# Reordering the second half of a dense feed-forward and the entry to the next attention layer, on all engines of a two-layer transformer kernel

## The reference

```
x = x + ffn(attention(x, ...))                    # layer 1
x = x + experts(attention(x, ...))                # layer 2

def attention(x, ...):                            # 16 heads of 64, one key and value for all heads
    xn = ln(x); q = xn @ Wq; k, v = split(xn @ Wkv)   # a null key and value are put in front
    sim = q @ k + bias, masked causally and by key
    return layernorm(softmax(sim) @ v @ Wout)

def ffn(x, ln1_g, ln1_b, w1, b1, ln2_g, ln2_b, w2, b2):
    h = layer_norm(x, ln1_g, ln1_b)
    h = h @ ternary_quant(w1).T + b1              # 128 -> 512
    h = gelu(h)
    h = layer_norm(h, ln2_g, ln2_b)               # over the 512
    return h @ ternary_quant(w2).T + b2           # 512 -> 128
```

## Time and profile before

| | before |
|---|---|
| time, median of 3 runs | 584.27 us (584.1 to 586.46) |
| span of the profiled execution, which is the time that its rows add up to | 586.0 us |
| mean granted TensorE clock | 0.934 |
| PE busy | 483.6 us (83%) |
| DVE busy | 426.4 us (73%) |
| ACT busy | 377.5 us (64%) |
| POOL busy | 312.0 us (53%) |

### The profile page before, as it was taken

The page is one execution under the profiler, slowest core; times in us unless marked ns, Lnnn a source line. Parts: engine busy times, 40 slices in busy tenths (PEclk is TensorE's granted clock), DMA queues, the critical chain, the costliest instruction groups (busy, mean ns, idle before and its releaser), DMA issues.

```text
span 586.0 us, 13781 instructions
## 1 busy us (share of the span) xinstructions
PE 483.6 (83%) x3220; PEld 390.9 (67%) x3220; DVE 426.4 (73%) x2148; ACT 377.5 (64%) x1475; POOL 312.0 (53%) x368
## 2 busy tenths in 40 slices
PE   3768999999999888987899999989987229999930
PEld 1456777777777676666788887867865217878730
DVE  4899999999999786577778888899887604343413
ACT  1568889888888866655888898868774004354410
POOL 4577666675657725567333453534675522555560
PEclk9689999999999989999899999999998659999975
DMA  5361016621100000000022120000111121323117
GB/s 170 93 180 22 20 26 137 141 78 45 41 4 6 8 3 2 0 1 7 6 65 58 44 77 5 8 7 15 37 38 31 40 68 36 84 53 83 36 38 215
DMA packets 54696, 29.73 MB, mean 51 GB/s; under 512 B 19884, under 2 KB 51572, under 8 KB 54644
## 3 DMA queue, kind: packets, MB, share of 16 engines
q1 hardware_dynamic: 48900, 22.09, 15.1%
q0 software_dynamic: 2560, 4.90, 2.6%
q10 hardware_dynamic: 3184, 2.16, 1.2%
HBM read 16.13 MB, written 10.90 MB: 46 GB/s over the span
## 4 chain that ended last, share of the span: by engine, by line
PE 59%; DVE 12%; issue 11%; POOL 6%; ACT 4%; DMA 4%; SPq 1%; another core or an unknown queue 1%; DVEq 0%; ACTq 0%; POOLq 0%
PE psS L863 10%; PE psA L918 7%; PE psS L1162 5%; PE psQ L834 4%; PE psT L881 4%; PE psO L899 4%; PE psQ L818 4%; PE psQ L1152 3%; PE psO L889 2%; DVE sc L1557 2%; PE psO L890 2%; DMA slot_rows<-Y,dest_u 1%; ACT qT L1248 1%; PE psO L1152 1%; PE psA L1152 1%
## 5 line engine op out<-in xcount | busy, mean ns | idle before, releaser
L1265 ACT ACTIVATE sc<-sc,negmax 128x97 f32<-128x97 f32 (+3 forms) x512 | 179.0, 354 | 23.7 <-DVE negmax L1557 22.1
L634 POOL TENSOR_TENSOR wide_buf<-bias,mask 128x132 f32<-128x132 f32 (+3 forms) x128 | 109.2, 877 | 9.2 <-DMA bias<-rel_scratch 3.9
L1557 DVE CUSTOM_DVE_ANT_0 sc<-psS,wide_buf 128x97 f32<-128x97 f32 (+3 forms) x512 | 93.6, 237 | 25.6 <-PE psS L863 18.4
L863 PE MATMUL psS<-kk,qT 128*128 128x194 f32 (+3 forms) x512 | 102.7, 322 | 11.6 <-DVE negmax L1557 11.6
L863 PEld LDWEIGHTS psS<-kk,qT 128*128 128x128 f32 x512 | 80.0, 195 | 33.0 <-issue 30.0
L1265 ACT ACTIVATION_READ_ACCUMULATOR sc<-sc,negmax 128x1 f32 x512 | 97.3, 190 | 0.0
L581 POOL TENSOR_TENSOR qrn<-qssc,half 128x9 f32<-128x9 f32 (+1 forms) x32 | 55.9, 1748 | 57.8 <-DVE qssc L1543 57.7
L1570 DVE TENSOR_TENSOR pn<-sc,rsum 128x128 f32<-128x128 f32 (+3 forms) x128 | 72.4, 566 | 6.8 <-DVE rsum L1566 0.2
L918 PE MATMUL psA<-Wo,OT 128*128 128x128 f32 (+1 forms) x512 | 65.7, 283 | 0.8 <-DVE OT L1582 0.8
L918 PEld LDWEIGHTS psA<-Wo,OT 128*128 128x128 f32 x512 | 62.7, 196 | 2.0 <-DVE OT L1582 1.8
L1582 DVE TENSOR_SCALAR OT<-psO,cols 128x512 f32<-128x512 f32 x64 | 47.6, 743 | 3.3 <-PE psO L899 1.8
(11 more groups left out here) (298 smaller groups left out, 1014.9 us busy)
## 6 DMA issues: line engine op xcount, KB each, us to landing
slot_rows<-empty SPq DMA_DIRECT2D x2, 1390.0 KB, 10.0
xb<-slot_rows SPq DMA_DIRECT2D x16, 139.0 KB
vp_u<-vp SPq DMA_DIRECT2D x128, 8.0 KB, 1.7
choice_rows<-zero_row SPq DMA_DIRECT2D x8, 256.0 KB, 3.2
wide_buf<-choice_rows SPq DMA_DIRECT2D x8, 256.0 KB, 5.0
vp_u<-vp SPq DMA_DIRECT2D x64, 16.0 KB, 1.8
eW<-in_L_ffn_W SPq DMA_DIRECT2D x4, 256.0 KB, 3.1
gT<-in_L_ffn_W SPq DMA_DIRECT2D x4, 256.0 KB, 3.0
```

The source lines that it names most:

```text
L634: pool.tensor_tensor(unit_masked(i, u).rearrange("p h e k -> p (h e) k"), unit_bias(layer, u).rearrange("p h e k -> p (h e) k"), mask[laye ...
L863: m = pe.matmul(score_bank(u, h), qT[i][:, h, u].rearrange("p m q -> p (m q)"), kk[i][:, :, 0:w], start=True, stop=True)
L1265: m = act.activation(v, v, ACT.Exp, bias=negmax[:, u, g:g + 1], scale=-1.0, accum_out=psum_row[:, u, g:g + 1])
L1557: dve.tensor_tensor_reduce(sc[u][:, h, e, :], score_bank(u, h)[:, e * WIDTH[u]:(e + 1) * WIDTH[u]], unit_masked(i, u)[:, h, e, :], -1.0, - ...
```

## The change

The same instructions are issued, on other tiles of PSUM in four cases, and in another order on four engines; SP's program is as before. By engine:
- PE: f_up(0, 1) to f_up(0, 3) and f_turn(1) are spread between the last projection of layer 1 and the two preparations. Of the last quad, two f_downs stay ahead of layer 2, f_down(14) goes behind b0's scores of u1 and f_down(15) behind those of u2; project_in for b1 follows it, turn_input for b2 comes behind u3. The last quad's tiles go to halves of psO and of one bank of psT, since psS then holds scores. A wait for all 16 reads stands ahead of b1's scores; the wait for 14 ahead of layer 2 is gone.
- ACT: f_in of the next quad one step earlier; in b0 the keys and queries of b1 behind u2's exponentials.
- DVE: dense_stats(3) ahead of the copies of the gate; f_norm_in(3) ahead of f_update(0); f_read(3) in two halves in b0's u2 and u3; f_update(3) and f_input_stats(3) in b1.
- POOL: the addition of c to X in four pieces spread through the program; the mask additions for b0 and f_input_rstd(0) ahead of quad 2's sums; the later f_input_rstds and f_scale(3) later.

```
 # PE
+            f_up(0, 1)
             project(0, NB - 1, 1, False)
...
+            f_up(0, 2)
+            pe.wait_ge(s["out_ready"], 2 * NB)
+            down_sums()
+            f_up(0, 3)
+            f_turn(1)
+            gate_fold()
...
             turn_input(1, 1, 1)
-            for t in range(NB - 4, NB):
-                f_down(t)
-            project_in(1, 1)
-            pe.wait_ge(s["f_o_read"], NB - 2)
+            f_down(NB - 4)
+            f_down(NB - 3)
 # PE, f_bank and f_down
+            if t >= NB - 4:
+                c = (t % 2) * (P + 2)
+                return (psO[:, c:c + P + 2], psT[:, 1, c:c + P + 2])[(t % 4) // 2]
...
-                held(pe, s["f_o_read"], t - 3)
+                held(pe, s["f_o_read"], t - 3 if t < NB - 4 else NB - 5 + (t % 4) // 2)
 # PE, batches of layer 2
+                    if no(b, 1):
+                        pe.wait_ge(s["f_o_read"], NB)
                     for u in range(UNITS):
                         scores(1, b, u, i)
+                        if first and u in (1, 2):
+                            f_down(NB - 3 + u)
+                        if first and u == 2:
+                            project_in(1, 1)
+                        if first and u == 3:
+                            turn_input(1, 2, 0)
 # ACT
+                    if j == FB - 1 and g < QUADS - 1:
+                        f_in(g + 1)
                     f_square(g, j)
-                if g < QUADS - 1:
-                    f_in(g + 1)
 # DVE
+            f_norm_in(2)
+            f_read(0)
+            f_norm_in(3)
+            f_update(0)
+            f_input_stats(0)
...
+                        if first and u == 2:
+                            values_in(1, 1, 1)
+                            f_read(QUADS - 1, 0, 2)
+                        if first and u == 3:
+                            f_read(QUADS - 1, 2, 4)
+                        if u == 1 and no(b, 1):
                             f_update(QUADS - 1)
-                        if first and u == 2:
+                        if u == 2 and no(b, 1):
                             f_input_stats(QUADS - 1)
 # POOL
+            f_pair_sum(0, 0)
+            f_shift(0)
+            f_pair_sum(0, 1)
+            f_square_sum(0)
             dense_rstd(QUADS - 1)
...
+            f_shift(1)
+            f_squares(1)
+            f_scale(0)
             pool.wait_ge(s["masks_ready"], 2)
             for u in range(UNITS):
                 mask_bias(1, 0, u, 0)
+            f_input_rstd(0)
+            f_squares(2)
+            f_shift(2)
+            f_scale(1)
+            f_squares(3)
+            f_scale(2)
             values_set(1, 0, 0)
...
+            f_shift(3)
+            f_input_rstd(1)
+            f_input_rstd(2)
```

More of the change, by code:

```diff
@@ L728, in f_input_rstd @@
                 rsqrt(rstd[:, 4 * g:4 * g + 4], ve[:, 4 * g:4 * g + 4], 4, s["x_rstd"])
+            f_pair_sum(0, 0)
+            f_shift(0)
+            f_pair_sum(0, 1)
+            f_square_sum(0)
             dense_rstd(QUADS - 1)
-            for g in range(QUADS):
-                f_squares(g)
-                if g:
-                    f_scale(g - 1)
-                if g and g < QUADS - 1:
-                    f_input_rstd(g - 1)
+            f_shift(1)
+            f_squares(1)
+            f_scale(0)
             pool.wait_ge(s["masks_ready"], 2)
@@ L1019, in batch @@
                             values(B - 1, 1 - i)
-                        if u == 2 and not last and not no(b, NB - 2):
+                        if u == 2 and not first and not last and not no(b, NB - 2):
                             turn_input(1, b + 2, i)
@@ L1101, in _ @@
             f_up(0, 0)
+            f_up(0, 1)
             project(0, NB - 1, 1, False)
-            for g in range(QUADS):
-                for j in range(FB):
-                    if g or j:
-                        f_up(g, j)
-                    if g == 0 and j == 0:
-                        pe.wait_ge(s["out_ready"], 2 * NB)
-                        down_sums()
-                    if g == 0 and j == 1:
-                        gate_fold()
+            f_up(0, 2)
[4 more added lines that the diff above has]
+            gate_fold()
+            for g in range(1, QUADS):
+                for j in range(FB):
+                    f_up(g, j)
                     if g == 1 and j == 1:
@@ L1116, in _ @@
                         f_turn(g + 1)
-                    if g and j:
+                    if j:
                         f_down(4 * (g - 1) + j - 1)
-                if g:
-                    f_down(4 * g - 1)
+                f_down(4 * g - 1)
             pe.wait_ge(s["y_done"], NB)
@@ L1329, in batch @@
                     for u in range(UNITS):
-                        if u == 0 and not last:
+                        if u == 0 and not first and not last:
                             keys_T(1, b + 1, 1 - i)
@@ L1336, in batch @@
                         weights(n + u, u)
-                        if u == 1 and not last:
+                        if u == 2 and first:
+                            keys_T(1, 1, 1)
+                        if u == (2 if first else 1) and not last:
                             queries(1, b + 1, 1 - i)
@@ L1949, in f_input_stats @@
                 dve.tensor_scalar(ve[:, quad], mv[:, quad, 1], LN_EPS, None, ALU.add).then_inc(s["x_var"], 1)
-            for g in range(QUADS - 1):
-                if g + 2 < QUADS:
-                    f_norm_in(g + 2)
-                if g == QUADS - 2:
-                    null_keys(cols[:, C_NK:C_NK + 1])
-                    dve.wait_ge(s["x_rstd"], 1)
-                    input_norm(1, 0, 0)
-                    input_norm(1, 1, 1)
-                f_read(g)
-                if g == QUADS - 2:
-                    values_in(1, 0, 0)
-                f_update(g)
-                f_input_stats(g)
-            f_read(QUADS - 1)
-            dve.wait_ge(s["x_rstd"], QUADS - 2)
+            f_norm_in(2)
[3 more added lines that the diff above has]
+            f_input_stats(0)
+            f_read(1)
+            f_update(1)
+            f_input_stats(1)
+            null_keys(cols[:, C_NK:C_NK + 1])
+            dve.wait_ge(s["x_rstd"], 1)
+            input_norm(1, 0, 0)
+            input_norm(1, 1, 1)
+            f_read(2)
+            values_in(1, 0, 0)
+            f_update(2)
+            f_input_stats(2)
             attention_second()
```

40 lines of the change are left out of this document (23 added, 17 removed).

## The result

| | before | after |
|---|---|---|
| median (lowest to highest) | 584.28 us (582.37 to 588.21), 20 runs | 580.07 us (578.42 to 586.48), 20 runs |
| ratio to before, 95% interval | | 0.994 (0.9921 to 0.9958) |
| span of the profiled execution, granted clock | 586.0 us, 0.934 | 578.3 us, 0.943 |

The change is 4.2 us faster by the medians, 3.5 by the ratio (2.5 to 4.6 by its interval); forecast were 3.2, and 581.0 us.

What follows compares the result with a forecast made beforehand. The prediction took PE's standing still or running slowly, in the feed-forward and b0, to be what counts. Its terms, 0 + 4.2 + 1.0 − 2.0, gave 3.2 us gained, 581.0 us on the median, range 578.0 to 584.8.

Steps and rivals of the forecast that it cites:

- Term 1: Feed-forward up to turn_input(1,0,0): 0; PE's closed holes are given back by POOL; bounds 3.1 gained to 0.4 lost.
- Term 2: From turn_input to b0's first scores: 4.2 us gained, as two f_downs and project_in(1) leave this stretch.
- Term 3: Batch b0: 1.0 us gained, moved work filling PE's idle time and the clock staying up; bounds 1.9 gained, 0.6 lost.
- Term 4: b1 and b2: 2.0 us lost, from f_update(3) and f_input_stats(3) on DVE in b1; bounds 0 to 2.9, or 4.3.
- Rival (c): Layer 2's entry: clock falls behind new PE holes of 1.7 and 2.4; 583.3, or 588.2 if through b0; chance 0.13.
- (a): Feed-forward and b1: update and masks overlap better, b1 absorbs half; gain 4.5 to 7 us, about 578.5; chance 0.22.

Runs made afterwards that it cites:

- e1: Changed kernel with only the new entry; the feed-forward on PE, ACT, DVE and POOL back in the old order; 584.13 us, 0.9996 of before.
- e7: Changed kernel plus matrix products nobody reads in PE's two waits, ahead of f_down(8)'s second product and b0's turn_input; 580.56 us, 0.9931 of before.
- e10: Kernel before plus 14 matrix products nobody reads in b0's PE wait of 3.99 us; 586.06 us, 1.0039 of before.
- e3: Changed kernel with b0's four mask additions on POOL behind quad 2's sums, f_input_rstd(0), f_scale(1) and a piece of X+c; 583.11 us, 0.9978 of before.
- e8: Changed kernel with f_update(3) moved on DVE from b1's to b2's u1 and f_input_stats(3) to b3's u1; 581.03 us, 0.9956 of before.
- e4: Changed kernel with f_down(12) ahead of b1's turn_input on PE and b0's queries ahead of b1's xnT on ACT; 580.92 us, 0.9933 of before.
- e5: e3 with null_keys and both input_norms ahead of f_update(1) on DVE, and values_in(b0) ahead of f_read(2); 579.34 us, 0.9916 of before.
- e6: e5 with f_input_stats(2) moved behind b0's second bias step and f_input_rstd(2) on POOL behind b1's values; 578.09 us, 0.9909 of before.
- e12: e6 with f_update(3) in b2, f_input_stats(3) in b3, and f_scale(3) on POOL behind b2's masks; 577.48 us, 0.9882 of before.

## Why the prediction was right, point by point

By the trace the mechanism stood in its main lines, and the sum of 3.2 met 3.7 by the trace and 4.2 by the medians. That it came so near is partly luck: terms 2, 3 and 4 were off by 0.8, 0.95 and 0.5, and the first offset half of the other two. And e1's median, with the same entry and no gain, leaves open why the medians show the whole. Term by term:

- Term 1, 0 forecast, 0.16 lost. Its steps are in the trace one by one: quad 3 begun 4.66 earlier (4.3 forecast), f_update(0) 3.02 under the masks (3.08), a wait of 1.87 for POOL's sum (1.7), turn_input at 39.69 after f_up(0,0) against 39.53. One step fell elsewhere: the 1.2 for quad 3's pair sums was not on f_update(1), which ran alone, but on the two xn (2.60 for 0.60), and the second hole was 0.88 and not 2.4, because the clock had fallen in the first. The page "SBUF — State Buffer" of the Trainium skill, section "Who interferes with whom", whose rule weighed for this end, was borne out: the four updates and the four masks took 3.02 and 3.09 side by side, as if in turns.
- Term 2, 4.2 forecast, 3.4 gained. The work that left was right; the 0.3 for PE reaching ACT's copies too soon was too small, the row shows 0.89, and its cause was not PE coming early but DVE's copy of the values coming late, behind the slow xn. e1 and e7, without that wait, have 5.42 and 5.53, just the 5.4 of the sum.
- Term 3, 1.0 forecast, 1.95 gained. The left-over waits were 0.31 and 0.24, not 0.8, and the clock stayed up, as assumed. e10 measures the clock's part by itself: 1.6. Against e10's b0 of 10.91 the 4.54 us of PE's work that moved into b0 cost nothing.
- Term 4, 2.0 lost by forecast, 1.23 in b1 and 0.25 in b2. The size was near, but the step that gave it failed. That the two pieces "now stand on DVE in b1, ahead of the bias steps of u2 and u3" is at most 0.48 of it by e3, and not what PE waits for at L919: e8 took them away and the wait stayed. f_scale(3), which the prediction counted among the pieces that lie "beside work of PE and DVE that doesn't wait for them", holds up the masks behind it on POOL.
- Rival (c) was half right. The clock did fall behind the new hole of 1.87 (1.92 for an L1119 of 1.05), but it was up again before the entry, and the slow products ran in what would have been turn_input's wait. That an idle stretch of PE puts it back to half rate is what the Trainium skill's page "TensorE: Matmul & The Clock Gate", section "Why this matters for your kernels", says; the trace agrees. e4 shows the case that (c) priced, with holes of 1.88 and 2.22 and a projection of 3.14 in the entry. That the profiled execution of the changed kernel was not of that kind was luck, though what it was worth is not shown: e4, with its own moves, starts b3 1.4 earlier all the same.
- A gain of (a)'s size was to be had, but not by this change: it needed xn ahead of f_update(1), as e5 and e6 show.

## What to carry to other kernels

When an engine's queue is rewritten to close one engine's holes, follow each moved piece to the next thing queued behind it on its own engine: here the masks cost by what they ran beside (f_update(0), then pn and xn), and f_scale(3) by the masks behind it, never by its own microsecond. Where f_input_rstd(3) was taken from ahead of the next masks, these came early and met pn. A hole is worth closing only if what waits at its end is early too; e3 closed one and merely lengthened the next, while one look at what xn(b0) needs gave 4.8 us of an earlier start. And a gain of 4 us in a 580 us kernel whose clock varies from run to run needs both readings, the stages counted from a point that no edit moves and the medians of many runs; either alone would have misjudged e1.

## What the runs showed of the hardware that was not expected

The stretch ahead of f_up(0,0), which no kernel here changes, took 220.6 to 222.8 us in twelve of the fourteen traces, at a granted clock of 0.90 to 1.00 from 205 to 222, and 225.4 and 225.6 in e5's and e4's, at 0.72. That stretch of e5, in the columns of the earlier trace rows:

```profile
205.00:222.00 17.00, 15.51 (x81) 13.32 (x80) 11.93 (x71) 9.59 (x44) 3.28 (x4) 0.72 0.01 3
```

So the same instructions cost up to 5 us more in one execution than in another, as much as the whole change. The kernels differ in how often: e12 kept a mean clock of 0.943 or more in six runs of six, before in 11 of the 29 beside it. Nor does the length of a wait decide alone: the 2.23 ahead of f_up(1,0) left the clock at 1.00 in the trace of before, and in e10's, where that part of the program is the same, the f_up(1,0) and f_up(1,1) behind it took 3.38 instead of 1.98. And DVE's xn, one 128x128 TENSOR_SCALAR, took from 0.34 to 1.42 according to what POOL did beside it.
